# The first expert's gates of a second expert stage: broadcast by TensorE instead of by a DMA

## What is computed

```python
def _L1_ffn_ref(hidden_states, Wg, W1, W3, W2):
    B, S, D, F, E, K = (4, 256, 128, 256, 8, 2)
    x = hidden_states.reshape(-1, d)
    gates = jax.nn.softmax(x @ Wg, axis=-1)
    top_g, top_i = jax.lax.top_k(gates, K)
    top_g = top_g / top_g.sum(axis=-1, keepdims=True)
    w = jnp.zeros((t, e), x.dtype).at[jnp.arange(t)[:, None], top_i].add(top_g)
    gate_h = jax.nn.silu(jnp.einsum('td,edf->etf', x, W1))
    up = jnp.einsum('td,edf->etf', x, W3)
    y = jnp.einsum('etf,efd->etd', gate_h * up, W2)
    out = jnp.einsum('te,etd->td', w, y)
    return out.reshape(b, s, d)
```

## Time and profile before

| | |
|---|---|
| median of 3 runs | 703.77 us (702.33 to 704.51) |
| profiled execution | 704.98 us |
| its span, first to last instruction | 703.2 us |
| mean granted TensorE clock in the span | 0.935 of full speed |

### The profile page before, as it was taken

How to read it: one execution, slowest core, us unless ns; L and a number is a source line. 1 busy time by engine, 2 the same in 40 slices (tenths; PEclk the granted TensorE clock), 3 DMA queues, 4 the chain that set the end, 5 groups by cost and what they waited for, 6 DMA issues and landing times.

```text
span 703.2 us, 11008 instructions
## 1 busy us (share of the span) xinstructions
PE 623.8 (89%) x3252; PEld 440.1 (63%) x3252; DVE 552.0 (79%) x1346; ACT 491.1 (70%) x849; POOL 176.6 (25%) x147
## 2 busy tenths in 40 slices
PE   8789989988997899999999998683698689999996
PEld 5355555555544668888888886342375468888884
DVE  2657888888866758888888888655899579999997
ACT  4548999999753669999999998278635146666663
POOL 4212222222401405443555434410133000000000
PEclk9779999999997799999999999786699789999999
DMA  7000000000000030222201220000000122223201
GB/s 231 1 0 1 2 2 1 0 0 0 31 1 0 5 150 6 85 91 90 89 11 78 89 82 0 23 1 0 0 1 0 41 105 83 89 98 110 93 1 60
DMA packets 6797, 30.90 MB, mean 44 GB/s; under 512 B 906, under 2 KB 1043, under 8 KB 4435
## 3 DMA queue, kind: packets, MB, share of 16 engines
q1 hardware_dynamic: 6756, 30.42, 12.0%
HBM read 29.23 MB, written 1.19 MB: 43 GB/s over the span
## 4 chain that ended last, share of the span: by engine, by line
PE 73%; DVE 17%; ACT 5%; issue 3%; DMA 2%; POOL 0%; DVEq 0%; SPq 0%; ACTq 0%; POOLq 0%
PE PS L1080 16%; PE PS L1082 16%; PE PS L1081 16%; DVE STAT L754 5%; PE PS L1195 3%; PE PS L1157 3%; PE PS L1177 3%; PE PS L1093 2%; PE PS L1191 2%; PE PS L1156 2%; PE PS L1222 2%; PE PS L1102 2%; PE PS L1231 2%; DVE HN L622 1%; DVE AR L1039 1%
## 5 line engine op out<-in xcount | busy, mean ns | idle before, releaser
L886 DVE TENSOR_TENSOR RA<-AR,RA 128x512 fp32r<-128x512 f32 x140 | 135.8, 995 | 29.2 <-ACT RA L493 28.4
L1080 PE MATMUL PS<-HH,WH 128*128 128x512 f32 x272 | 109.7, 403 | 7.3 <-DVE AR L1031 7.2
L492 ACT ACTIVATE AR<-PS,BI 128x512 f32<-128x512 f32 x144 | 99.5, 691 | 23.7 <-PE PS L1082 14.0
L1081 PE MATMUL PS<-HH,WL 128*128 128x512 f32 x272 | 108.1, 398 | 0.0
L1082 PE MATMUL PS<-HL,WH 128*128 128x512 f32 x272 | 107.9, 397 | 0.0
L493 ACT ACTIVATE RA<-PS,BI 128x512 fp32r<-128x512 f32 x144 | 98.4, 684 | 0.0
L754 DVE CUSTOM_DVE_ANT_0 STAT<-PS,MQ 128x128 f32<-128x128 f32 (+1 forms) x256 | 76.3, 354 | 22.0 <-PE PS L1178 21.5
L297 POOL TENSOR_TENSOR AR<-AR 128x512 f32<-128x512 f32 x36 | 56.4, 1566 | 120.8 <-DVE AR L709 120.5
L1080 PE MATMUL PS<-RA,WH 128*128 128x512 f32 x208 | 83.3, 401 | 2.5 <-DVE RA L1046 2.0
L1081 PE MATMUL PS<-RA,WL 128*128 128x512 f32 x208 | 81.7, 393 | 0.0
L1082 PE MATMUL PS<-RA,WH 128*128 128x512 f32 x208 | 81.7, 393 | 0.0
(11 more groups left out here) (184 smaller groups left out, 1195.5 us busy)
## 6 DMA issues: line engine op xcount, KB each, us to landing
AR<-comb SPq DMA_DIRECT2D x17, 1024.0 KB, 4.7
WS<-in_w SPq DMA_DIRECT2D x9, 512.0 KB, 5.5
WS<-in_w SPq DMA_DIRECT2D x8, 384.0 KB, 3.1
M<-in_mats SPq DMA_DIRECT2D x1, 1384.0 KB, 10.7
X<-in_xT SPq DMA_DIRECT2D x4, 256.0 KB, 4.2
out_xT<-X SPq DMA_DIRECT2D x4, 256.0 KB, 2.1
AR<-in_wmod SPq DMA_DIRECT2D x1, 768.0 KB, 7.7
KM<-in_kmats SPq DMA_DIRECT2D x1, 160.0 KB, 8.0
```

Source lines behind the costliest of these rows:

```text
L492: act.activation(G[:, c, :], PS[:, c, :], ACT.Gelu_apprx_tanh, bias=bias).then_inc(s["act"], 1)
L886: dve.tensor_tensor(out=GL[:, m0 % 2, c, :], in0=G[:, c, :], in1=f(GH[:, m0 % 2, c, :]), op=ALU.subtract).then_inc(s["lo"], 1)
L1080: pe.matmul(out, wh, xh, start=first, stop=False)
L1081: pe.matmul(out, wl, xh, start=False, stop=False)
```

## The change

In the second expert stage, expert 0's gates no longer pass through DRAM. `first_gates(t)` on PE does four matmuls for a block: the stationary operand is the column COMB[:, i, 0:1], read 128 times with a step of 0, and the moving operand is the identity IDF, so that all 128 output partitions get the 128 tokens' gates. They land in bank 4 + t, which output1 fills later. ACT copies the bank into WB[:, 0] (`copy_gates`). The transposed rows are still made for the other experts, but ACT copies them too (`copy_rows`) in place of DVE, and the transposes of blocks 2 and 3 and the gate matmuls of blocks 2 and 3 are moved in between the first expert matmuls. SP loads only expert 1's row at first. weigh1 waits for the gate copies for expert 0. The first expert stage keeps its way.

```diff
                 sp.wait_ge(s["stored"], 16)
-                for e in range(2):
+                for e in range(n, 2):
                     sp.dma_start(WB[:, e, :], comb[e:e + 1, :].to_broadcast([128, TOK])).then_inc(s[f"wb_in{e}"], 16)
...
+            def copy_gates(t):
+                act.wait_ge(s1["gate_psum"], t + 1)
+                act.activation(WB[:, 0, t * BLK:(t + 1) * BLK], PS[:, 4 + t, :], ACT.Copy)                   .then_inc(s1["first_gates"], 1)
+
+            def copy_rows(t):
+                act.wait_ge(s1["combT"], t + 1)
+                act.activation(CT[0:E1, t * BLK:(t + 1) * BLK], PS[0:E1, 6 + t % 2, :], ACT.Copy)                   .then_inc(s1["ct"], 1)
+
             silu(0, 0)
             for m in range(4 * E1):
                 silu(m, 1)
+                if m == 0:
+                    copy_gates(0)
+                    copy_rows(0)
+                    copy_gates(1)
                 upper1(m, 0)
+                if m == 0:
+                    copy_rows(1)
                 if m + 1 < 4 * E1:
                     silu(m + 1, 0)
+                if m < 2:
+                    (copy_rows, copy_gates)[m](2)
                 upper1(m, 1)
+                if m < 2:
+                    (copy_rows, copy_gates)[m](3)
...
             route(1, E1)
-            routes_in(1, E1)
             s1 = moe[1]
...
             def weigh1(m, c):
                 e, t = m // 4, m % 4
-                if t == 0 and c == 0:
-                    dve.wait_ge(s1[f"wb_in{e % 2}"], 16 * (e // 2 + 1))
+                if e == 0:
+                    dve.wait_ge(s1["first_gates"], t + 1)
+                elif t == 0 and c == 0:
+                    dve.wait_ge(s1[f"wb_in{e % 2}"], 16 * ((e + 1) // 2))
...
+            def first_gates(t):
+
+                if t >= 2:
+                    pe.wait_ge(s1["ct"], t + 1)
+                else:
+                    pe.wait_ge(s1["comb"], 1)
+                for i in range(4 * t, 4 * t + 4):
+                    mm = pe.matmul(PS[:, 4 + t, 128 * (i % 4):128 * (i % 4) + 128],
+                                   COMB[:, i, 0:1].to_broadcast([128, 128]), IDF[:, :], start=True, stop=True)
+                mm.then_inc(s1["gate_psum"], 1)
+
             def output1(m, c):
...
-                if e == 0 and c == 0 and t >= 2:
-                    pe.wait_ge(s1["ct"], 1 + t)
+                if e == 0 and c == 0:
+                    pe.wait_ge(s1["first_gates"], t + 1)
...
-            for t in range(NBLK):
+            for t in range(2):
+                first_gates(t)
                 route_out(1, E1, t)
             for m in range(4 * E1):
                 for c in range(2):
                     if m + 1 < 4 * E1:
                         hidden1(m + 1, c)
+                    if m == 0:
+                        route_out(1, E1, 2 + c)
+                    elif m == 1:
+                        first_gates(2 + c)
                     if m > 0 or c > 0:
                         output1(m - (c == 0), 1 - c)
```

More of the change, by code:

```diff
@@ L160, in moe_sems @@
             names = ("logits", "lg", "exps", "rstep", "comb", "combT", "ct", "stored", "b2_psum", "acc_init",
-                     "w_in", "split", "wb_in0", "wb_in1", "h", "act", "prod", "gh", "lo", "y", "ymul", "acc")
+                     "gate_psum", "first_gates", "w_in", "split", "wb_in0", "wb_in1", "h", "act", "prod", "gh", "lo", "y", "ymul", "acc")
             return {k: sem(f"moe{n}_{k}") for k in names}
@@ L693, in route @@
                     dve.memset(COMB[:, :, 8:9], 1.0).then_inc(s["comb"], 1)
-            def routes_in(n, ne):
-                s = moe[n]
-                for t in range(NBLK):
-                    dve.wait_ge(s["combT"], t + 1)
-                    dve.tensor_copy(CT[0:ne, t * BLK:(t + 1) * BLK], PS[0:ne, 6 + t % 2, :]).then_inc(s["ct"], 1)
             def moe_scale(s, m, m0, pair):
@@ L873, in _ @@
             s = moe[0]
-            routes_in(0, E0)
+            for t in range(NBLK):
+                dve.wait_ge(s["combT"], t + 1)
+                dve.tensor_copy(CT[0:E0, t * BLK:(t + 1) * BLK], PS[0:E0, 6 + t % 2, :]).then_inc(s["ct"], 1)
             def bias_sum(t):
```

## The result

The changed kernel takes 696.16 us (median of 4 runs, 695.22 to 697.07) against 703.21 us of the kernel before (4 runs, 702.33 to 704.51): a ratio of 0.9898, 95% interval 0.9876 to 0.9920. Two later sets of runs of the same two kernels gave 696.73 against 702.66 (ratio 0.9920, 0.9898 to 0.9942) and 697.63 against 703.57 (0.9917, 0.9902 to 0.9933). So it is faster by 5.9 to 7.1 us; 6.2 was forecast.

The account below looks back on a forecast made before the run. TensorE's order, behind expert 0's DMA round trip, bounds the kernel; gates, transposes and 30 expert matmuls sum to output1(1, 0) at 567.22 against 573.40 us, so 703.77 - 6.2 = 697.6 us, range 695.3 to 701.0.

Parts of the forecast that it names:

- The path: TensorE's work from COMB to output1(1, 0), summed from 553.20 to 567.22 us against 573.40: a gain of 6.2 us.
- first gate group: First four gate matmuls on TensorE behind COMB, eight records at the 1.2 GHz level: 1.70 us.
- The stationary operand with a step of 0: Gate matmuls on TensorE: assumed to cost what other fp32 records do, 0.21 us or 0.115 us each by clock.
- Rival A: Gate matmuls expose their weight loads, 0.46 us a record: slower by 3.6 us, 707.4 us; chance 4%.
- The dearer price, 0.21: Us per gate record at the 1.2 GHz level, from 14 records at program start; 0.115 at full clock.
- The clock: TensorE behind COMB: granted clock 0.50 from 553.3 to 556.6 us as before, 1.00 behind it.
- rival B: The low clock behind COMB lasts longer, to 560.0 or 563.4: gain 4.5 or 2.8 us; chance 12%.
- the second slow stretch: Low clock behind the 559.9 to 565.6 gap, 11 matmuls at 0.427 instead of 0.227 us: 2.2 us, forecast to go.
- ScalarE in order: Eight copies of about 0.60 us on ScalarE cost nothing; tightest cover 0.7 us, silu(2, 1) behind the fourth gate copy.
- Rival C: ScalarE's copies delay silu(2, 1) and silu(1, 1), holding hidden1 up to 1 us: gain 5.2, 698.6 us; chance 8%.
- SP's queue: Store and broadcast of expert 1's gates land at about 568.7 us, needed at 575.4: 6.7 us to spare.
- rival D: No gain: the wait moves to expert 1's gates, or weigh1(0, 0) still waits for a transfer; chance 2%.

Follow-up runs that it names:

- e6: Changed kernel with eight unread 512-column matmuls filling TensorE's gap ahead of the first gate group: 694.81 us, ratio 0.9882 to the kernel before.
- e4: Changed kernel with each gate matmul replaced by a transpose of the same column, one record instead of two: 695.12 us, ratio 0.9867 to the kernel before.
- e3: Changed kernel with every gate matmul done twice, same result: 701.01 us, ratio 0.9963 to the kernel before.
- e5: Kernel before with 24 unread 512-column matmuls filling TensorE's wait for the gates' DMA: 702.52 us, ratio 0.9991 to the kernel before.
- e8: Changed kernel run again without any edit: 696.73 us, ratio 0.9920 to the kernel before.
- e11: Changed kernel run a third time without any edit: 697.63 us, ratio 0.9917 to the kernel before.
- e2: Changed kernel with the four row copies kept on VectorE and all 16 transposes ahead of hidden1(1, 0): 699.29 us, ratio 0.9930 to the kernel before.

## Why the prediction was right

**The path.** The step that carried the number was the sum on TensorE from COMB to output1(1, 0): 6.2 us forecast, 6.3 measured. Its terms against the pieces of the chain: first gate group 1.70, measured 1.98; its transposes 0.69, measured 0.85; second group 1.41, measured 1.29; transposes 0.52, measured 0.44; the later transposes 1.04, measured 0.88; the later gate groups 1.86, measured 1.78. Both columns add up to 7.22 us, and that they agree so well is luck: single terms were off by up to 0.28 us, the first two came out longer, all others shorter. The first group contains the start of a first matmul behind a wait, which the sum had left out: at full clock throughout, in e6, the first group took 1.16 us and the second 0.89. The first product starts at 551.26, just as COMB is written, and the first weigh1 at 554.05, 2.7 us behind COMB where 2.6 was forecast (555.8 for a COMB at 553.2).

**The stationary operand with a step of 0** costs nothing: eight records in 0.89 us are 0.11 each, against 0.115 taken from the 64-row form. Rival A is out. e4 adds that the number of stationary columns, 8 or 128, does not matter either. The dearer price, 0.21, was read from matmuls at the start of the program on the argument that their slowness was the clock's. The view of the granted clock does not show that (it gives 1.00 from 1.1 to 4.5 us), so the prediction had no row for it; what bears it out is the stretch behind COMB, where e3's 16 records took 3.68 us at a granted clock of 0.50.

**The clock** behaved as assumed, low for about 3.4 us behind the gap ahead of COMB and high from then on; rival B did not come. e5 puts the second slow stretch at 2.1 us of the change's 6.3, 2.2 forecast.

**ScalarE in order.** The tightest place was where it was said to be, silu(2, 1) behind the fourth gate copy:

```profile
565.57 0.60 ACT L598 ACTIVATE AR<-PS 128x512 f32<-128x512 f32 x1 [1.85 <-PE PS L1490]
...
566.06 0.59 ACT L583 ACTIVATE AR<-PS 128x512 f32<-128x512 f32 x1
...
566.69 0.69 DVE L1044 TENSOR_TENSOR AR<-PS,AR 128x512 f32<-128x512 f32 x1 [1.65 <-ACT AR L583]
...
568.12 0.39 PE L1095 MATMUL PS<-HH,WH 128*128 128x512 f32 x1
```

product1(2, 1) ends at 567.38 and hidden1(3, 1) starts at 568.12: cover 0.7 us, as computed. Rival C did not come.

**SP's queue.** The broadcast of expert 1's gates is issued at 562.72 and takes 4.4 us, so the gates are there at 567.1; weigh1(4, 0) starts at 573.87. That is 6.8 us to spare, 6.7 forecast; rival D did not come.

**The total.** The median moved by 7.05 us in the first set, 5.9 in the two others. The measured 696.16 lies 1.4 us below the forecast of 697.6: 0.56 because the median of before, over four runs, was 703.21 and not 703.77, the rest is within the scatter of the runs. No step of the sum accounts for it. By the traces the change is worth 6.1 us to the end of the span, which lies inside the 5.9 to 7.1 of the three sets.

## What to carry to other kernels

When a wait on the path is a transfer that only reshapes a small result, ask which engine stands idle through it and what it could do in the same time. Then sum that engine's own list from the event that releases it, at the clock that it will have: each record counts, as e3 and e4 show in both directions. And measure such an edit by a distance between two events of the trace around it, because the medians here scatter by more than parts of it are worth.

## What the runs showed of the hardware that was not expected

- A gap of only 2 us in TensorE's work was followed by 3.4 us at the 1.2 GHz level in all three profiles of the changed kernel (the first, e8, e11). The last matmuls ahead of the gap had run at full clock, but for little more than 1 us (in the first profile the granted clock rose at about 548.1, and the gap began at 549.4). With eight matmuls in the gap (1.98 us) the clock stayed at 1.00 in all three profiles that had them. A gap of 1.46 us further on, in e2 and in e5, was not followed by the lower level.
- An fp32 record of 128 moving columns cost 0.11 us with 8 or with 128 stationary columns, read with a step of 0 or not (0.44 us for four, both ways); at the lower level 0.21.
- Whole executions of one kernel differed by up to 6.3 us (the kernel before over all sets: 699.35 to 705.68 us). Between the profile of before and that of the changed kernel 2.1 us arose by 41 us of the program; in all fourteen profiles the spread at that point was 3.3 us.
